# A first cross attention whose scores move through a ring of three PSUM banks, with bank-wide maxima

## The reference, cut to what matters

```python
q = (x1 @ Wq + bq)                       # 128 queries, 16 heads of 8
k = concatenate([x2 @ Wk + bk, ctx])     # 128 + 120 = 248 keys
v = concatenate([x2 @ Wv + bv, ctx])
attn = softmax(q k^T * 8 ** -0.5)        # per head
x = layernorm(x1 + (attn @ v) @ Wp + bp)
gate_out = x @ gate_w                    # logits of 8 experts, for the stage behind
```

## Time and profile before

| | us |
|---|---|
| median of 3 runs | 2766.59 (2761.22 to 2768.04) |
| the profiled execution | 2770.02 |
| its span on the core | 2768.2 |
| first cross attention within it, from the first S product to the last T product | 492.4 to 1185.2 |
| 62 steps of it, from the second turned maxima to the last | 518.9 to 1176.7 |

### The profile page before, as it was taken

One profiled execution on the slowest core, in us unless ns is written; L12 is line 12 of the kernel. 1 busy time (PEld: TensorE's weight loads), 2 busy tenths in 40 slices (PEclk: granted clock), 3 DMA queues, 4 the chain that ended last, 5 costly groups with the idle time before them and its releaser, 6 DMA issues. The chain is left out here.

```text
span 2768.2 us, 95705 instructions
## 1 busy us (share of the span) xinstructions
PE 2516.4 (91%) x29950; PEld 2005.2 (72%) x29951; DVE 1814.5 (66%) x5178; ACT 1735.1 (63%) x6375; POOL 1396.5 (50%) x2914
## 2 busy tenths in 40 slices
PE   7999997899999999969888869999999799999995
PEld 6888886566666666648667757888888688888884
DVE  3555565566666666655333447888888488888886
ACT  4666664355555555412555647888888578888883
POOL 2333332233333333336676446777777266666664
PEclk9999999799999999979999989999999899999997
DMA  6323233111111111113232211111111111111100
GB/s 157 99 82 88 81 88 78 39 44 44 44 41 45 40 45 39 31 56 104 71 78 73 66 58 46 52 51 51 51 48 43 33 29 33 33 30 30 31 27 10
DMA packets 270160, 151.37 MB, mean 55 GB/s; under 512 B 51776, under 2 KB 263744, under 8 KB 270016
## 3 DMA queue, kind: packets, MB, share of 16 engines
q1 hardware_dynamic: 261312, 131.57, 17.8%
q0 software_dynamic: 8704, 17.97, 1.8%
HBM read 92.52 MB, written 48.51 MB: 51 GB/s over the span
## 5 line engine op out<-in xcount | busy, mean ns | idle before, releaser
L1576 ACT ACTIVATE pr<-psT 120x512 f32<-120x512 f32 (+1 forms) x512 | 277.9, 595 | 302.7 <-PE psT L1483 302.7
L1186 ACT ACTIVATE pr<-psS,small 128x128 f32<-128x128 f32 x1024 | 365.9, 383 | 96.0 <-DVE small L1257 93.4
L1621 DVE TENSOR_REDUCE small<-psS 128x4 f32<-128x992 f32 x256 | 303.5, 1186 | 93.4 <-PE psS L1487 93.4
L1473 PE MATMUL psT<-cross_Qm,cross_xf 32*120 32x512 f32 (+1 forms) x1024 | 307.4, 643 | 48.0 <-DVE cross_xoT L1669 43.5
L1186 ACT ACTIVATION_READ_ACCUMULATOR pr<-psS,small 128x1 f32 x1024 | 226.2, 221 | 0.0
L2163 POOL DMA_INDIRECT results<-experts_ob,experts_xb x144 | 138.5, 962 | 116.3 <-ACT experts_ob L1983 103.2
L1257 DVE TENSOR_REDUCE small<-psS 128x8 f32<-128x1024 f32 x128 | 156.8, 1225 | 61.6 <-PE psS L1151 61.6
L1478 PE MATMUL psS<-cross_xf,cross_Qm 32*128 32x248 f32 x1024 | 194.0, 430 | 0.9 <-DVE small L1621 0.9
L2103 DVE SCALAR_TENSOR_TENSOR experts_bgh<-experts_bth,psS 128x256 f32<-128x256 f32 x144 | 60.7, 421 | 199.1 <-ACT experts_bth L1975 199.1
L955 POOL TENSOR_SCALAR pr<-pr,small 128x120 f32<-128x120 f32 x512 | 179.1, 366 | 23.9 <-DVE small L909 23.9
L813 ACT ACTIVATE pr<-psS,small 128x120 f32<-128x120 f32 x512 | 178.6, 389 | 5.4 <-DVE small L928 5.4
(11 more groups left out here) (318 smaller groups left out, 7763.4 us busy)
## 6 DMA issues: line engine op xcount, KB each, us to landing
self_parts<-results SPq DMA_DIRECT2D x64, 192.0 KB, 2.4
slots<-blank SPq DMA_DIRECT2D x18, 520.0 KB, 4.7
experts_xb<-slots SPq DMA_DIRECT2D x144, 65.0 KB, 1.9
self_near<-in_x SPq DMA_DIRECT2D x128, 64.0 KB, 1.9
between<-self_xo SPq DMA_DIRECT2D x128, 64.0 KB, 1.6
cross_x<-between SPq DMA_DIRECT2D x128, 64.0 KB, 1.8
cross_res<-between SPq DMA_DIRECT2D x128, 64.0 KB, 1.8
self_x<-in_x SPq DMA_DIRECT2D x64, 64.0 KB, 1.8
```

Of the source, the lines that this page charges most:

```text
L1186: last = act.activation(pr[e.slot % 4][:, cols], K.S[e.slot % 2][:, cols], ACT.Exp, bias=nmax[e.slot % 4][:, n:n + 1], accum_out=tot[k.slo ...
L1473: pe.matmul(T[0:size, 512 * n:512 * n + 512], xf[t.slot][rows(g), every][:, places[ck]], Qm[t.slot][rows(g), :], start=True, stop=False)
L1576: act.activation(PT[k][0:sizes[ck], half], T[0:sizes[ck], half], ACT.Exp).then_inc(exped, 1)
L1621: dve.tensor_reduce(out, src, AX.X, ALU.max, negate=True).then_inc(maxed, 1)
```

## The change

S and T each get a ring of three banks. `psS` becomes one tensor of four banks; its first three are S's ring, the two banks of `psT` and the last bank of `psS` are T's. A step has eight halves h = 2r + n, and half h goes to the bank `turn[h]` of both rings; `before[h]` is the half that used the bank last, whose maximum and exponential TensorE waits for. Since eight isn't a multiple of three, halves 0 and 1 follow halves 6 and 7 of the step before, one round behind them; all others follow a half three or five behind (h - 3, or half 5 of the step before). The maxima are taken half by half, eight instructions a step instead of four.

The turned maxima, the logits and the turned result go to `W0`. The turned maxima take all of it, so they are placed behind the first `weigh`, where the projections have just been read, and have to be copied out before the turned input is written. VectorE's order follows: the scaling of the sums stands ahead of the values, the copy `NB` ahead of the second round's maxima, the logits and the turned result behind them. TensorE no longer waits for `NB` ahead of a round, but ahead of its second part; and it waits for `turned_sb` of z ahead of the projections at the end of the step, no longer ahead of round 2.

```diff
-    K.S = [K.ctx.enter_context(K.nc.psum_tensor(f"psS{i}", [P, 1024], F32)) for i in range(2)]
+    K.SS = K.ctx.enter_context(K.nc.psum_tensor("psS", [P, 2048], F32))
+    K.S = [K.SS[:, 0:1024], K.SS[:, 1024:2048]]
...
+    S = [K.SS[:, 512 * i:512 * i + 512] for i in range(3)]
+    T = [K.T[:, 0:512], K.T[:, 512:1024], K.SS[:, 1536:2048]]
+    turn = (0, 1, 2, 0, 1, 2, 0, 1)
+    before = (6, 7, 5, 0, 1, 2, 3, 4)
...
-                        need(pe, maxed, c.done(R, r - 1) if r >= 2 else (c - 1).done(R, r + 3))
-                        if r == 2:
-                            need(pe, nb_sb, (c - 1).done())
-                            need(pe, turned_sb, (c - 5).done())
...
                         if t.live:
-                            need(pe, exped, t.done(2 * R, 2 * k - 1 + n) if k else (t - 1).done(2 * R, 2 * R - 1 + n))
+                            h0 = before[h]
+                            of, k0, _, _, _, _ = round_of(c if h0 < h else c - 1, h0 // 2)
+                            need(pe, exped, of.done(2 * R, 2 * k0 + h0 % 2 + 1))
...
                         if c.live:
+                            need(pe, maxed, (c if before[h] < h else c - 1).done(2 * R, before[h] + 1))
...
                     scores(c, 0)
                     weigh(c - 2, 0)
-                    scores(c, 1)
...
+                    if w.live:
+                        need(pe, summed, w.done())
                     if m.live:
                         need(pe, split, m.done(5))
                         for j in range(J):
-                            last = pe.matmul(S[0][:, P * j:P * j + P], diag[m.slot % 2][:, P * j:P * j + P], K.identb[:],
+                            last = pe.matmul(W0[:, P * j:P * j + P], diag[m.slot % 2][:, P * j:P * j + P], K.identb[:],
                                              start=True, stop=True)
                         last.then_inc(nb_ps, 1)
+                    scores(c, 1)
+                    if m.live:
+                        need(pe, nb_sb, m.done())
+                    if a.live:
+                        need(pe, x_in[a.slot], a.p * 32 + 32)
+                        pe.transpose(W0[:, 0:P], x[a.slot][:], K.ident[:]).then_inc(in_ps, 1)
...
-                        need(dve, S_ps, c.done(2 * R, 2 * r + 2))
                         need(dve, split, (c - 2).done(5))
-                        out = nmax[c.slot % 2][:].rearrange("p (g j) -> p g j", g=G)[:, sg[0]:sg[0] + 2, j0:j0 + 2]
-                        src = S[r % 2][:].rearrange("p (g j k) -> p g j k", g=2, j=2)[:, :, :, 0:CTX + P]
-                        dve.tensor_reduce(out, src, AX.X, ALU.max, negate=True).then_inc(maxed, 1)
+                        for n in range(2):
+                            need(dve, S_ps, c.done(2 * R, 2 * r + n + 1))
+                            src = S[turn[2 * r + n]].rearrange("p (j k) -> p j k", j=2)[:, :, 0:CTX + P]
+                            dve.tensor_reduce(nmax[c.slot % 2][:, J * sg[n] + j0:J * sg[n] + j0 + 2], src, AX.X, ALU.max,
+                                              negate=True).then_inc(maxed, 1)
```

More of the change, by code:

```diff
@@ L1469, in scores @@
                     for n in range(2):
-                        g = tg[n]
+                        h = 2 * r + n
+                        g, to = tg[n], T[turn[h]]
                         if t.live:
-                            need(pe, exped, t.done(2 * R, 2 * k - 1 + n) if k else (t - 1).done(2 * R, 2 * R - 1 + n))
-                            pe.matmul(T[0:size, 512 * n:512 * n + 512],
-                                      xf[t.slot][rows(g), every][:, places[ck]], Qm[t.slot][rows(g), :],
+                            h0 = before[h]
+                            of, k0, _, _, _, _ = round_of(c if h0 < h else c - 1, h0 // 2)
+                            need(pe, exped, of.done(2 * R, 2 * k0 + h0 % 2 + 1))
+                            pe.matmul(to[0:size, :], xf[t.slot][rows(g), every][:, places[ck]], Qm[t.slot][rows(g), :],
@@ L1479, in scores @@
                                       xf[c.slot][rows(g), every], start=True, stop=True)
                     for n in range(2):
-                        g = tg[n]
+                        h = 2 * r + n
+                        g, to = tg[n], T[turn[h]]
                         if t.live:
-                            pe.matmul(T[0:size, 512 * n:512 * n + 512], onesb[rows(g), 0:size], NB[t.slot % 2][rows(g), :],
+                            need(pe, nb_sb, t.done())
+                            pe.matmul(to[0:size, :], onesb[rows(g), 0:size], NB[t.slot % 2][rows(g), :],
@@ L1556, in step @@
                         need(pe, oT_sb, n.done())
+                    if z.live:
+                        need(pe, turned_sb, z.done())
                     if a.live:
@@ L1573, in exps @@
                         for n in range(2):
-                            half = slice(512 * n, 512 * n + 512)
                             need(act, T_ps, t.done(2 * R, 2 * k + 1 + n))
-                            act.activation(PT[k][0:sizes[ck], half], T[0:sizes[ck], half], ACT.Exp).then_inc(exped, 1)
+                            act.activation(PT[k][0:sizes[ck], 512 * n:512 * n + 512], T[turn[2 * r + n]][0:sizes[ck], :],
+                                           ACT.Exp).then_inc(exped, 1)
                 def step(c):
@@ L1646, in step @@
                                           r[:, :, 3:4].to_broadcast([P, G, HD]), ALU.mult).then_inc(scaled, 1)
+                    if b.live:
+                        need(dve, proj_ps, b.done())
+                        need(dve, qk_sb, b.done(2))
+                        need(dve, O_ps, (b - 4).done(G))
+                        put(Vx[b.slot][:, 1], W0[:, 2 * P:3 * P], dve, K.rowb[:, 0, :]).then_inc(v_sb, 1)
                     if w.live:
@@ L1659, in step @@
                         need(dve, nb_ps, m.done())
-                        dve.tensor_copy(NB[m.slot % 2][:], S[0][:, 0:512]).then_inc(nb_sb, 1)
+                        dve.tensor_copy(NB[m.slot % 2][:], W0[:]).then_inc(nb_sb, 1)
+                    maxima(c, 1)
                     z, v = c - 5, c - 6
+                    if a.live:
+                        need(dve, in_sb, a.done())
+                    if n.live:
+                        need(dve, oT_ps, n.done())
                     if z.live or v.live:
@@ L1703, in step @@
                         s = m.slot % 2
-                        need(pool, maxed, m.done(R))
+                        need(pool, maxed, m.done(2 * R))
                         need(pool, nb_ps, (m - 2).done())
```

59 lines of the change are left out of this document (21 added, 38 removed).

## The result

The changed kernel takes 2697.74 us (median of 4 runs, 2695.52 to 2697.93) against 2763.9 for the kernel before (2759.33 to 2768.04): a ratio of 0.9759, interval 0.974 to 0.9778. Run again later beside other kernels it took 2697.29 against 2765.24, a ratio of 0.9757 (0.9736 to 0.9778). The forecast was 2707 in a range of 2694 to 2748; the gain is 66 to 68 us where 60 were forecast. The experiments ran on three chips; each ratio is to the kernel before on the same chip.

A forecast was written before the change was run, and what follows sets the result against it. TensorE's own queue was taken to bound the stage. A step of 10.61 us falls to 9.48 without waits, plus 0.10 and small S lateness 9.63; 0.98 times 62 steps is 61 us, giving 2707 us, range 2694 to 2748.

The forecast's parts named there:

- What bounds the stage: TensorE's own queue sets the step, busy 90%; only its idle time, 1.02 us a step, and its switches can be saved.
- the forecast of over 97% busy: Sign in the changed profile: TensorE busy over 97% of the stage.
- The no-wait sum of 9.48 us: One step shown in the trace, 10.70 us, less TensorE's two waits, 1.22 us, is 9.48 us.
- The turned maxima alone, 0.10: Between `weigh` and round 1 the turned maxima take 0.33 us of TensorE instead of 0.23: cost 0.10 a step.
- The wait of round 2: Ahead of round 2, TensorE's wait for the copy of the turned result, 0.82 us in the step shown, goes.
- The step on the copy to `NB`: VectorE copies the turned maxima until 3.55 us into the step; the transposes want it at 3.90: cover 0.35.
- The wait of `weigh`: Ahead of the first `weigh`, TensorE's wait for VectorE's scaling, 0.40 us in the step shown, goes; cover 0.3 to 0.4.
- The rings: T's longer distance takes away 2.5 us of idle time; halves other than 0 and 1 have three halves' distance.
- S one round behind: S halves 1 and 5 start about 0.25 us late, mostly hidden by T; 0.02 to 0.03 counted for each.
- The late S ring: S halves 1 and 5 stretch rounds 0 and 2, 0.3 to 0.6 us a step, about 2735 us; chance 0.26.
- The given-back case: A wait of the same size for `NB` ahead of the transposes replaces round 2's; about 2764 us, chance 0.06.
- The slower one: At round starts TensorE's queue works out its waits, 0.1 us each, 1.2 a step, 2777 us; chance 0.08.

The follow-up runs named there:

- the short exponential: Kernel before with ScalarE's second exponential of round 2 covering 256 of its 512 columns in the 52 looped steps: 2762.7 us, ratio 0.9981.
- the two delays: Changed kernel with two or five idle VectorE reductions ahead of half 7's maximum: 2834.74 us (ratio 0.9837) and 2872.14 us (0.9974), on another chip.
- the first two experiments: Changed kernel with T in its old pair: without S's ring and halved maxima 2729.36 us (ratio 0.9874), with both kept 2738.47 us (0.9899).
- the one that waits for `NB`: Changed kernel with the turned maxima back behind round 1, ahead of the small products: 2879.04 us, ratio 0.9985, on another chip.

## Why the prediction was right, point by point

*What bounds the stage.* Right: TensorE's own queue, with 1.02 us idle a step. The result is that queue without idle time, and the forecast of over 97% busy was 99.9%. As a sign it was weak: the kernels in which a T or S half waits 0.3 to 0.9 us a step are above 99% too.

*The no-wait sum of 9.48 us.* Mis-sized, by about 0.2, of which 0.07 came back in another place. It took the length of each block as work. Round 3 held 0.10 us of waiting for the exponential in T's pair of banks, which is no idle time, as one of four tiles waits while the others run; the short exponential shows it. Round 2, 1.37 before, held another 0.10: behind its wait the second T half started 0.11 after the first (827.78, 827.89), although the exponential ahead had ended at 827.25; what for is open. A round of 120 keys whose halves start together takes 1.27 to 1.28. The term is 9.28 in that step, and 9.38 with the turned maxima alone. Measured was 9.45. The missing 0.07 is round 2 of the changed kernel, 1.34:

```profile
809.91 0.60 ACT L1577 ACTIVATE pr<-psS 128x512 f32<-128x512 f32 x1 [1.53 <-PE psT L1485]
```

```profile
810.48 0.69 PE L1473 MATMUL psT<-cross_Qm,cross_xf 32*120 32x512 f32 x1
...
810.56 0.69 PE L1473 MATMUL psS<-cross_Qm,cross_xf 32*120 32x512 f32 x1
```

Half 5 takes the bank of half 2, whose exponential ends at 810.51. The T half starts 0.05 behind it, as in every case above, and 0.08 behind its neighbour. This is so in three looped steps of four. In the fourth the small products take 0.76 instead of 0.66, the exponential ends 0.07 before round 2 begins, the halves start 0.01 apart (801.10, 801.11), and the round takes 1.27. So even T's ring of three is a little short there; the rows say so, no run changed it by itself.

*The turned maxima alone, 0.10.* Right: 0.33 us. The Trainium skill's rule that a change of tiling mode drains the engine (TensorEngine Tiling (Array Packing), Key Properties) is no further cost here: `weigh` to turned maxima to round 1 go 1.01 and 0.33 from start to start, as the rows of before gave for such changes.

*The wait of round 2.* It went, and nothing came late in its place but the 0.08 of half 5 told above. The step on the copy to `NB` held with less cover than laid out: the copy started 3.02 us after round 0 and not 2.86, as VectorE stands 0.12 us between the end of its statistics and the copy, and it ended at 809.63, 0.19 before the transposes want it, where 0.35 were named.

*The wait of `weigh`.* It went. It was worth 0.33 us a step in the changed kernel, where the prediction had 0.40 for the step in its rows, on the long side of the average; the average idle of 16.8 / 61.3 and 0.07 give 0.34.

*The rings.* The prediction's conclusion held, its attribution did not. It said that T's distance "takes away the 2.5 us" of the earlier trace rows. It takes away 32 us, because the other edits pull rounds 1 and 2 to 1.94 us from each other, while an exponential pair is done 2.45 us after its round began. (Rounds 0 and 1 lie 2.62 apart, which is enough.) And "all other halves have three halves' distance" is not quite enough at half 5, as just said. With the old pair, nearly half of what the other edits bring is given back there. I had worked out what the rings cost and never what their absence would cost in the new order. It made no difference to the sum, only because the rings were in it.

*S one round behind.* Right: the last maximum ends 0.13 us into the next round 0 (806.05; 0.12 laid out), the S half starts 0.17 late (0.25 laid out; the signal takes 0.05 and not 0.1), and the cover is 0.25 (0.23 from the rows). So round 0 pays nothing; I had taken 0.02 to 0.03. In round 2 the S half is 0.20 late (0.25 laid out), within the cover too. A half is 0.669 us (0.67). VectorE's busy time, 475.85 / 61.2 = 7.8 us a step, is the 7.8 laid out, by luck: the halves add 0.26 us of busy time and not 0.6, as the kernel before with half maxima shows, and the other 0.3 came with the new order. The kernel without rings or halves has 442.53 us in 580, 7.6 a step. `split` ends at 807.80, 1.88 into the step (1.83).

*The rivals.* The late S ring: its mechanism is real, as the two delays show, and stood 0.08 us away. The given-back case is what the kernel with the turned maxima behind round 1 does. The slower one, a queue that works out its waits in sight, isn't seen: in rounds 0 and 1 each half of T and of S now has a wait of its own, and their T halves still start 0.01 apart and the rounds take the same 1.28 us as before. The 0.08 in round 2 looks like that rival's sign, but the fourth step, with the same instructions and 0.01, speaks for the exponential.

*From the step to the time.* 0.98 x 62 = 61 was 1.14 x 62 = 70.6 in the trace, and 66 to 68 between medians. Stages that are the same in both kernels differ by some us from one program to the next, as between the first two experiments. The forecast of 2707 was 9 us too long, which is the 0.16 us a step between 9.63 and 9.47: waits counted as work, and a lateness of the S halves that cost nothing.

## What to carry to other kernels

A wait removed brings the next round nearer, and what was far enough behind before may not be now: work out for every buffer what its distance must be in the new order, not in the old one. When several tiles of TensorE run side by side, a wait of one of them is no idle time; compare the start times of the tiles in a round, and the length of the same block in different places. And the worth of an edit depends on the others: the scaling's place is 0.13 us or 0.33, T's third bank some 0.1 in the kernel before (an estimate from the short exponential) or 0.51.

## What the runs showed of the hardware

The granted clock can fall for a few microseconds in the middle of a stage that is 1.00 otherwise. With the wait ahead of round 2, which leaves TensorE idle 1.2 us in every step, it did so ten times in 62 steps:

```profile
706.00:711.00 5.00, 3.77 (x62) 2.46 (x58) 4.44 (x13) 2.33 (x5) 2.02 (x7) 1.00 0.23 65
711.50:714.80 3.30, 3.30 (x45) 2.14 (x37) 1.51 (x3) 1.08 (x2) 0.73 (x2) 0.50 0.00 0
715.00:720.00 5.00, 5.00 (x78) 3.74 (x74) 3.30 (x11) 3.17 (x7) 1.89 (x6) 1.00 0.20 56
```

The columns are those of the earlier trace rows; 0.50 is the 1.2 GHz level. Each fall lasts 3.4 us and costs 1.56: the step takes 12.56 instead of 11.0. The one shown begins some 0.6 us after the idle time before round 2 had ended (710.85 in the rows of that experiment). In the kernel before, with idle times of 0.33 and 0.75 us in the step shown, and in the one that waits for `NB`, with 0.86, the clock of the looped steps is 1.00. What decides between them was not tried.

The copy L1665 starts 0.12 us after the end of the instruction ahead of it, on whose own semaphore a wait stands between them, while VectorE's instructions without such a wait overlap by 0.08: there the wait for the engine's own last result costs 0.2 us of its time. At the scaling, which waits for the reciprocal ahead of it, the gap is 0.03 (806.23, 806.26), so 0.11.

One chip ran the kernel before in 2765 us and another in 2881; of the second there are profiles of four other kernels. In them the clock of this stage is 1.00 too but in the experiment just told, and the time is lost behind the stage: with two idle reductions, 2833.2 - 1127.8 = 1705 us follow the last copy, against 2695.8 - 1102.1 = 1594 for the changed kernel on the first. The mean granted clock of these stretches is 0.93 against 0.96. Whether the clock is the cause or only goes with it is open.
